# Cross-attention and a ternary feed-forward on one core: the key projections of a head leave PSUM as whole 128-partition tiles into a staging tile, and DMAs carry their halves to their places

## The reference

```python
q_hk = (hidden_q @ Wq.T).reshape(Bv, Sv, H, K)            # H = 16 heads, K = 128
q_big = jnp.einsum('bshk,hkq->bshq', q_hk, w_kc_q)        # 384 wide
q_big = _apply_rope(q_big, sin_q, cos_q)
kv_r = _apply_rope(kv_c, sin_k, cos_k)                    # 2 batches x 1024 rows x 128
q_r = jnp.einsum('bshq,hqr->bhsr', q_big, W_qr)           # R = 64
k_r = jnp.einsum('bld,hdr->bhlr', kv_r, W_kr)             # keys: 64 per head
scores = jnp.einsum('bhsr,bhlr->bhsl', q_r, k_r)
attn = jax.nn.softmax(scores, axis=-1)
ctx_c = jnp.einsum('bhsl,bld->bhsd', attn, kv_r)
ctx_lat = jnp.einsum('bhsd,hkd->bhsk', ctx_c, w_kc_kv)
...
return ctx @ Wo.T
```

## Time and profile before

| what | value |
|---|---|
| median of 3 runs | 858.98 us |
| profiled execution, span from first to last instruction | 861.5 us |
| PE busy | 757.3 us (88%) |
| DVE busy | 766.2 us (89%) |
| ACT busy | 573.6 us (67%) |
| POOL busy | 577.6 us (67%) |
| DMA | 118.50 MB, mean 138 GB/s |
| TensorE's granted clock, mean | 0.966 |

### The profile page before, as it was taken

How to read it: one execution, slowest core, us unless ns; L and a number is a source line. 1 busy time by engine, 2 the same in 40 slices (tenths; PEclk the granted TensorE clock), 3 DMA queues, 4 the chain that set the end, 5 groups by cost and what they waited for, 6 DMA issues and landing times.

```text
span 861.5 us, 12578 instructions
## 1 busy us (share of the span) xinstructions
PE 757.3 (88%) x3268; PEld 487.1 (57%) x3268; DVE 766.2 (89%) x1026; ACT 573.6 (67%) x838; POOL 577.6 (67%) x581
## 2 busy tenths in 40 slices
PE   3678998989999999999999999999999675868996
PEld 3555565756666666666566656665666442424543
DVE  5799899989998999899989999999999767797895
ACT  2477677767766867687667766776777576774332
POOL 5769674867486757766776668576848474867462
PEclk9889999999999999999999999999999797889999
DMA  9216867776768576858676766677668999400000
GB/s 330 79 49 115 169 130 140 138 167 134 151 114 170 117 161 132 170 111 167 118 160 134 152 128 138 149 137 150 125 146 213 241 227 275 164 0 25 13 24 37
DMA packets 294405, 118.50 MB, mean 138 GB/s; under 512 B 271856, under 2 KB 278000, under 8 KB 294128
## 3 DMA queue, kind: packets, MB, share of 16 engines
q1 hardware_dynamic: 293568, 116.68, 62.0%
q10 hardware_dynamic: 816, 1.57, 0.5%
HBM read 49.02 MB, written 2.10 MB: 59 GB/s over the span
## 4 chain that ended last, share of the span: by engine, by line
PE 35%; POOL 20%; DVE 18%; issue 11%; DMA 7%; SPq 5%; ACT 3%; POOLq 1%; DVEq 0%; ACTq 0%
PE banks L1419 22%; POOL rot_cos L1055 5%; PE scores L1720 5%; DMA load<-in_pack 4%; POOL rot_lo L1063 4%; SPq L943 4%; PE scores L1507 3%; PE banks L1735 3%; DVE neg_max L1323 3%; POOL rot_hi L1061 2%; DVE rows L1330 2%; POOL rot_sin L1046 2%; DVE rot_cos L1295 2%; DVE cv_lo L1288 1%; POOL wq_lo L388 1%
## 5 line engine op out<-in xcount | busy, mean ns | idle before, releaser
L1185 ACT ACTIVATE scores<-scores,neg_max 128x1024 f32<-128x1024 f32 x128 | 139.2, 1087 | 56.1 <-DVE neg_max L1323 54.6
L1330 DVE SCALAR_TENSOR_TENSOR rows<-scores,rows 128x1024 f16<-128x1024 f32 x128 | 154.9, 1220 | 13.7 <-ACT rows L1196 12.6
L1419 PE MATMUL banks<-pt,v_hi 128*128 128x512 f16 x512 | 154.3, 383 | 12.5 <-DMA pt<-rows 11.4
L1323 DVE TENSOR_REDUCE neg_max<-scores 128x1 f32<-128x1024 f32 x128 | 155.5, 1216 | 2.9 <-PE scores L1507 2.7
L1055 POOL TENSOR_TENSOR rot_cos<-rot_cos,rot_sin 128x512 f32<-128x512 f32 x93 | 119.2, 1281 | 46.6 <-DVE rot_sin L1297 42.2
L1196 ACT ACTIVATE rows<-scores 128x1024 f16<-128x1024 f32 x128 | 130.8, 1022 | 5.2
L1063 POOL TENSOR_TENSOR rot_lo<-rot_cos,rot_hi 128x512 fp32r<-128x512 f32 x93 | 119.6, 1286 | 7.8
L1159 ACT CAST cv_hi<-banks 128x512 fp32r<-128x512 f32 x64 | 37.6, 587 | 102.6 <-PE banks L1419 101.4
L1318 DVE SCALAR_TENSOR_TENSOR acc<-banks,inv,acc 128x512 f32<-128x512 f32 x128 | 91.4, 745 | 8.0 <-PE banks L1419 4.1
L1419 PE MATMUL banks<-pt,v_lo 128*128 128x512 f16 x256 | 97.8, 382 | 0.0
L1419 PEld LDWEIGHTS banks<-pt,v_hi 128*128 128x128 f16 x512 | 44.5, 98 | 79.2 <-issue 36.4
(11 more groups left out here) (211 smaller groups left out, 1824.7 us busy)
## 6 DMA issues: line engine op xcount, KB each, us to landing
load<-in_pack SPq DMA_DIRECT2D x15, 320.0 KB, 3.5
raw_chunk<-in_out_w SPq DMA_DIRECT2D x8, 512.0 KB, 5.2
raw_chunk<-in_gate_w SPq DMA_DIRECT2D x8, 512.0 KB, 4.4
raw_chunk<-in_val_w SPq DMA_DIRECT2D x8, 512.0 KB, 4.6
raw<-in_gate_w SPq DMA_DIRECT2D x8, 512.0 KB, 5.5
raw<-in_val_w SPq DMA_DIRECT2D x8, 512.0 KB, 5.2
raw<-in_out_w SPq DMA_DIRECT2D x8, 512.0 KB, 7.0
load<-in_pack SPq DMA_DIRECT2D x15, 256.0 KB, 3.3
```

What stands on the lines that cost most here:

```text
L1185: nc.scalar.activation(scores[:, u % 2, :], scores[:, u % 2, :], ACT.Exp, bias=neg_max[:, u:u + 1], accum_out=sums[:, u:u + 1]).then_inc(e ...
L1323: nc.vector.tensor_reduce(neg_max[:, u:u + 1], scores[:, u % 2, :], AX, ALU.max, negate=True).then_inc(max_ready, 1)
L1330: nc.vector.scalar_tensor_tensor(out=rows[:, u % ROWS, 1, :], in0=scores[:, u % 2, :], scalar=WEIGHT_LIFT, in1=rows[:, u % ROWS, 0, :], op ...
L1419: mm = nc.tensor.matmul(out, ws[a], xs[c], start=first and n == 0, stop=last and n == 2)
```

## The change

ScalarE's part of a K group is one copy of all 128 partitions into `stage[:, 0, :]`, DVE's is one subtraction of 128 partitions into `stage[:, 1, :]`. Then SP issues four DMAs of 64 x 512 float32 (128 KB each) that carry the upper and lower halves of both parts to `kr_even` and `kr_odd`, and count `keys_placed` up by 64 per group. The opening period keeps the old form.

`stage` lies on the same bytes as `raw_chunk`, so chunks and keys take turns: K(0,0)'s copy waits until the chunk before is summed, the copies of K(0,1), K(1,0) and K(1,1) wait until the keys of the group before are in place, and chunk 1 waits until those of K(1,1) are. The sums move: chunks 1 and 2 are now in the even period, chunk 0 in the odd one. The scores of an even head wait on `keys_placed` instead of `group_read`.

The diff, cut to its core:

```diff
@@ ODD_PE
-    ("B", 1, 1, "next"), ("score", 5), part(0, 8, V0), part(1, 8, V0), part(2, 8, V0), part(3, 8, V0),
-    ("K", 0, 0, "next"), part(4, 8, V0), ("K", 0, 1, "next"), part(5, 8, V0), ("B", 1, 2, "next"), part(6, 8, V0),
+    ("K", 0, 0, "next"), ("B", 1, 1, "next"), ("score", 5), part(0, 8, V0), part(1, 8, V0), part(2, 8, V0), part(3, 8, V0),
+    ("K", 0, 1, "next"), part(4, 8, V0), part(5, 8, V0), ("B", 1, 2, "next"), part(6, 8, V0),
@@ EVEN_ACT
-    ("B", 0, 2, "next"), V1, ("exp", 2), ("high", 2), ("exp", 3), ("double", 1, "last"), ("high", 3), A1, ("abs", 2),
+    ("B", 0, 2, "next"), V1, ("exp", 2), ("high", 2), ("abs", 1), ("exp", 3), ("double", 1, "last"), ("high", 3), A1,
...
-    ("exp", 6), ("high", 6), ("exp", 7), C1,
+    ("abs", 2), ("exp", 6), ("high", 6), ("exp", 7), C1,
@@ ODD_ACT
-    ("exp", 5), ("high", 5), ("K", 0, 0, "next"), ("K", 0, 1, "next"), ("B", 1, 2, "next"), V0, ("double", 0, "next"),
-    ("exp", 6), ("high", 6), ("abs", 1), ("exp", 7), C1,
+    ("K", 0, 0, "next"), ("exp", 5), ("high", 5), ("K", 0, 1, "next"), ("B", 1, 2, "next"), V0, ("double", 0, "next"),
+    ("exp", 6), ("high", 6), ("exp", 7), C1,
@@ ODD_DVE
-    ("B", 1, 1, "next"), ("max", 5), C0, ("low", 4), ("low", 5), ("K", 0, 0, "next"), ("K", 0, 1, "next"),
+    ("B", 1, 1, "next"), ("max", 5), C0, ("low", 4), ("K", 0, 0, "next"), ("low", 5), ("K", 0, 1, "next"),
@@ EVEN_SP
-    ("turn", 7, "last"), ("lot", 2), ("lot", 3), ("chunk", 0), ("turn", 0), ("turn", 1), ("turn", 2), ("turn", 3),
-    ("turn", 4), ("turn", 5), ("lot", 0), ("turn", 6), ("lot", 1),
+    ("keys", 1, 0), ("turn", 7, "last"), ("lot", 2), ("keys", 1, 1), ("lot", 3), ("chunk", 1), ("turn", 0), ("turn", 1), ("turn", 2),
+    ("turn", 3), ("chunk", 2), ("turn", 4), ("turn", 5), ("lot", 0), ("turn", 6), ("lot", 1),
@@ ODD_SP (LATE_SP, for head 14, changes like EVEN_SP)
-    ("turn", 3), ("turn", 4), ("chunk", 1), ("lot", 0), ("turn", 5), ("lot", 1), ("turn", 6),
+    ("turn", 3), ("turn", 4), ("keys", 0, 0), ("lot", 0), ("turn", 5), ("keys", 0, 1), ("lot", 1), ("turn", 6),
@@ attention_heads
+        stage = nc.alloc_sbuf_tensor_at("stage", [P, 2, S], F32R, offset=nc.sbuf_top)
+        def keys_before(h, n):
+            return h.pairs(256) - 512 + n
@@ load_chunk
+                if h.number and w == 1:
+                    sp.wait_ge(keys_placed, keys_before(h, 256))
@@ sync_heads
+            def place_keys(p, item):
+                _, b, half = item
+                h, marked = (p.head, item) if b else (p.head.plus(1), (*item, "next"))
+                marked = ("K", *marked[1:])
+                sp.wait_ge(group_read, p.emptied_at(marked))
+                if h.i is not None:
+                    sp.nop(nofuse=True)
+                upper, lower = slice(0, R), slice(R, 2 * R)
+                up, down = (x[:, b, half * 512:(half + 1) * 512] for x in (kr[half], kr[1 - half]))
+                for into, k, out_of in ((up[upper], 0, upper), (down[lower], 0, lower), (up[lower], 1, upper),
+                                        (down[upper], 1, lower)):
+                    sp.dma_start(into.bitcast(F32), stage[out_of, k, :].bitcast(F32)).then_inc(keys_placed, 16)
@@ high_part (ScalarE)
+                elif kind == "K" and not p.first:
+                    h = owner(p, marked)[0]
+                    act.wait_ge(summed, chunk_number(p.head, 1))
+                    if group[1] or group[2]:
+                        act.wait_ge(keys_placed, keys_before(h, 128 * group[1] + 64 * group[2]))
+                    act.nop(nofuse=True)
+                    out = stage[:, 0, :]
@@ take_out (VectorE)
+                    if kind == "K" and not p.first:
+                        return nc.vector.tensor_tensor(stage[:, 1, :], src, stage[:, 0, :].bitcast(F32), ALU.subtract)
@@ score_tile (TensorE)
-                if not odd:
-                    here = b or p.first
-                    pe.wait_ge(group_read, p.read(*(p.place(("K", b, half)) if here else p.earlier(("K", 0, half, "next"))
-                                                    for half in range(2))))
+                if p.first:
+                    pe.wait_ge(group_read, p.read(*(p.place(("K", b, half)) for half in range(2))))
+                elif not odd:
+                    pe.wait_ge(keys_placed, keys_before(p.head, 256 if b else 128))
```

More of the change, by code:

```diff
@@ L74 @@
 A0, A1, V1, V0, C0, C1 = ("A", 0, "next"), ("A", 1, "next"), ("V", 1, "last"), ("V", 0), ("C", 0, "next"), ("C", 1, "next")
-UNGROUPED = ("score", "max", "exp", "sum", "double", "abs", "drop", "stats", "spread", "root", "deviation", "norm", "extreme", "scale", "X", "take", "first root",
+UNGROUPED = ("keys", "score", "max", "exp", "sum", "double", "abs", "drop", "stats", "spread", "root", "deviation", "norm", "extreme", "scale", "X", "take", "first root",
              "turn", "start root", "values", "count", "variance", "inverse", "normed", "rotate", "products", "rotated",
@@ L189 @@
 LATE_SP = (
-    ("turn", 7, "last"), ("lot", WRK), ("turn", 0), ("lot", WVO), ("chunk", 0), ("turn", 1), ("turn", 2), ("turn", 3),
-    ("raw", 0, 0), ("raw", 0, 1), ("raw", 1, 0), ("turn", 4), ("raw", 1, 1), ("raw", 2, 0), ("raw", 2, 1),
+    ("keys", 1, 0), ("turn", 7, "last"), ("lot", WRK), ("keys", 1, 1), ("chunk", 1), ("turn", 0), ("lot", WVO), ("turn", 1),
+    ("turn", 2), ("chunk", 2), ("turn", 3), ("raw", 0, 0), ("raw", 0, 1), ("raw", 1, 0), ("turn", 4), ("raw", 1, 1), ("raw", 2, 0), ("raw", 2, 1),
     ("turn", 5), ("raw", 3, 0), ("turn", 6), ("raw", 3, 1),
@@ L840, in attention_heads @@
         inv_ready = sem("inv_ready")
-        chunk_loaded, summed = sem("chunk_loaded"), sem("summed")
+        chunk_loaded, summed, keys_placed = sem("chunk_loaded"), sem("summed"), sem("keys_placed")
         partial_ready, gamma_made = sem("partial_ready"), sem("gamma_made")
@@ L971, in period @@
                             turn_row(p, item)
-                    elif item == ("chunk", 0):
+                    elif item[0] == "chunk":
                         if not p.first:
-                            load_chunk(p.head, 0 if odd else 2)
-                    elif item == ("chunk", 1):
-                        load_chunk(p.head, 1)
+                            load_chunk(p.head, item[1])
+                    elif item[0] == "keys":
+                        if not p.first:
+                            place_keys(p, item)
                     elif item[0] == "pair":
```

## The result

The changed kernel took 931.44 us (median of 4 runs, 929.34 to 936.1), the kernel before 858.49 beside it (856.54 to 860.82): recorded ratio 1.0832, interval 1.0797 to 1.0866 (the two medians divided give 1.0850, inside it). Forecast were 916, with 878 to 945 as the range. The profiled execution spans 928.0 us, 66.5 more than that of before.

A forecast was written before the change was run, and what follows sets the result against it. TensorE and VectorE were taken as nearly full, 2 to 3.5 us free per period. 7 x (4.6 + 2.3) = 48.3, with the clock 57.3 on the 861.5 span: 918.8; that span being 2.5 above the median, forecast 916, range 878 to 945.

The forecast's parts named there:

- the three waits: V(0) for a bank and K(0,1) for landed keys (odd period), turn 7 behind K(1,0)'s keys (even period).
- The odd term: Odd period: ScalarE's copy of K(0,1) waits for K(0,0)'s landed keys, O(0) late by 4.6 us, bounds 3.2 and 8.6.
- the 3 to 4 that the prediction named as a sign: Odd period: ScalarE would stand some 3 to 4 us on the key DMAs before copying K(0,1).
- The bank wait alone: Odd period: V(0) waits for C(0)'s bank, +1.9 us; as a rival, only this is left: 872 us, chance 0.1.
- The even term: Even period: turn 7 behind K(1,0)'s keys, and K(1,1)'s copy awaiting them, delay V(1)'s take-out 2.3 us, bounds 1.2 and 5.5.
- The clock: TensorE's granted clock falls after the new stops, counted at three of the seven V(1): 9 us.
- The rival that the clock falls at nearly every new stop: TensorE at the stops before V(0) and V(1): 28 us on the 48, 935 us; 930 to 965, chance 0.17.
- low clock in most pairs: Sign that the prediction is wrong: TensorE's granted clock is low in most pairs of heads.
- Short landings: Key DMAs and turn 7 come at the lower bounds, clock holds: 31 us, 890 us; 880 to 900, chance 0.2.
- VectorE is the bound: Shorter VectorE work decides, DMAs beside it: 11 us in all, 848 us, or 840; faster had chance 0.05.
- the added bytes cost by themselves: The 2 MB more per pair, some 7 us of DMA engines busy 0.7 of the time, were put at no cost.

## Why the prediction was right, and where its sizes were off

**The direction and the three waits** were right, each in its place: the bank before V(0), the landed keys before K(0,1) and K(1,1), turn 7 before V(1). That the saved work is worth next to nothing was right too: the prediction left 0.69 us of K(1,1) on the chain; without the DMAs and in the old order six of seven pairs were 0.4 to 0.5 us shorter, and 22 us less of VectorE gave a ratio of 0.997 to 1.000.

**The odd term**, +4.6. Four DMAs of 128 KB took 4.56 us from first issue to last landing in the period shown, 4.6 to 4.9 in all seven, where the prediction had 4.6 from a 512 KB chunk. That the numbers meet is in part luck: the chunk is one issue, while of the four the last is issued 2.1 us behind the first and lands 2.4 later. The Trainium skill (DMA: Bandwidth & Descriptors, "Anatomy of one DMA") had given an estimated 3.6; it has the figure for DMAs that GpSimd issues, and here SP issues them. Its 2.0 us plus bytes, an estimated 2.3, nearly holds for one of these DMAs, 2.4 us by the median, but its 0.3 us for each further one misses the 0.59 to 0.60 that SP takes to issue each. O(0) came 5.1 us later instead of 4.6, mostly because the first key DMA left 0.4 us later than put, turn 4 taking 1.98 us and not 1.76. ScalarE stood 7.3 us before K(0,1), not the 3 to 4 that the prediction named as a sign, though the time of the landing was nearly right.

**The bank wait alone**, +1.9, was mis-sized, and a part of the miss is in the sum itself. By its own numbers C(0)'s bank comes free 0.6 us later than before (455.2 for 454.6), the first four parts of V(0) take 2.6, and K(0,0), already done, saves 0.69. That makes 2.5; the +1.9 lacks the 0.6. Measured were 2.5 us for the stop (forecast 3.1 us of standing, measured 3.32). The larger part is the clock behind it, 1.7 to 2.9, which I had counted as mostly hidden. It is hidden in the changed kernel, where the keys are due later (V(0) has time to be slow), and in the open as soon as they are not: 890 instead of the rival's 872. The single terms don't add. Bank and clock are 4.0 to 4.2, the landed keys over them only some 1.4 more, 5.6 in the mean.

**The even term**, +2.3. V(1) was 2.7 us late instead of 2.3: the four issues put turn 7 off by 2.6 us, where I had 1.7, and the transpose landed after 4.45 instead of 5.0. These two errors are of opposite sign. The 4.45 is the 4.4 of the transposes before: the key DMAs made this one start late, not run long. Less the 0.4 of slack it is 2.3, where the prediction had 1.9 for this path and took its 2.3 from the path through K(1,1); that the forecast number is met is luck. Turn 7 is the one that decides: without any wait for landed keys the even period stayed at 42.7 to 43.5.

**The clock**, 9 us on three of the seven V(1) at 3 us each. Here the prediction was wrong about how often: it fell at all seven, for 3.4 us with 1.7 lost, twice for 6.8 with 3.2. In the even period of head 8, 2.7 less 0.4 of slack and 1.66 of clock make the 3.95 by which V(1)'s low part was late.

**The sum.** Odd 7 x 5.6 = 39 and even 7 x 4.5 = 31.5, with the clock in both, is 70.6 instead of the forecast 57.3. Of these 13.3 us the odd periods make 6.9 (39.1 for 32.2) and the even ones with their clock 6.4 (31.5 for 25.1). The opening period is 0.9 longer, its start 0.9 earlier, and what follows the last max 0 is 4.0 us shorter (180.7 instead of 184.7); with these it is 66.6 of the measured 66.5. The shorter end is hardly the change's: it is 179.0 to 183.2 in all the kernels profiled here but the one before, and 180.7 in the kernel before with one order changed. All other runs took 1.8 to 3.4 us more than their span, so the profiled execution of before, with a span of 861.5, was probably a long one, of some 864 us. That would explain the 2.5 us by which the prediction found it above the median. From median to median the kernel lost 73 us, and the periods account for 70.6 of them.

**The rivals.** The rival that the clock falls at nearly every new stop (935, with 930 to 965 at 0.17) is what came: 931.44 lies in its band and not in the 900 to 930 that had 0.45, and low clock in most pairs was among the prediction's own signs of being wrong. It had its size wrong, 3 us for a fall where most cost 1.7. Short landings are out by the 4.6 to 4.9 us. That VectorE is the bound is out by the two kernels that save 11 and 22 us of it for nothing. The bank wait alone is real, but worth 30 to 36 us and not 13. That the added bytes cost by themselves, which the prediction had put at nothing, was tried and is out, as far as copies to HBM can stand for half of them.

## What to carry to other kernels

An engine that is 89% busy is not thereby the bound: count what its instructions are waited for, not what they add up to. A result that is needed at once must not pass through a queue whose every small DMA takes 0.6 us to issue and 2.4 to land, least of all ahead of a transpose on which TensorE waits; half as many behind it, with half a period until somebody wants them, were free. Before a group is moved in a kernel whose banks go round, write down which bank each later group gets: one place cost 4% here.

## What the runs showed of the hardware that I had not expected

TensorE's granted clock fell from its full 2.4 GHz to 1.2 at the stop of 3.3 us before V(0), within 1.3 us of its end on either side, in all seven odd periods of two kernels (the order alone, and the one without the DMAs), yet in 5 of 7 with K(0,0) and K(1,0) staged: the same stop, once with 1.7 us behind it and once without. All low stretches of the pairs were 3.4 or 6.8 us long. In the kernel before, where the longest stop of TensorE in the pairs is 1.1 us, there is none in them.

A DMA of 64 x 512 float32 within SBUF keeps SP for 0.58 to 0.61 us when it follows another one, against 0.33 to 0.53, median 0.36, for 32 KB of weights; one of the whole 128 x 1024 tile to HBM kept it for 0.58 to 0.59 and landed after 3.1. The Trainium skill (DMA: Bandwidth & Descriptors, "Rules for kernel authors") advises against two transfers to disjoint partition halves; here four quarters took 2.4 to 3.0 us of SP and 4.1 to 4.9 to land, one whole tile 0.6 and 3.1, so the runs agree, though the whole one went to HBM, and the halves have different places to go to.
